# A decoder layer on one core: four banks shared by row maxima and scores, all heads' scores as one group, and a new order of work on every engine

## The reference

```python
x = _layernorm(x + _L0_attn_ref(x, L0_attn_W_q, L0_attn_W_kv, L0_attn_W_o), axis=-1)
x = _layernorm(x + _L0_xattn_ref(x, ctx_2048, ctx_2048), axis=-1)
x = _layernorm(x + _L0_ffn_ref(x, L0_ffn_weight, L0_ffn_rram_variation), axis=-1)
```

## Time and profile before

| | us |
|---|---|
| median of 3 runs | 259.92 (259.2 to 260.36) |
| the profiled execution | 258.83 |
| its span, first to last instruction | 257.0 |
| TensorE busy | 197.5 (77%) |
| VectorE busy | 164.8 (64%) |
| GpSimd busy | 126.8 (49%) |
| ScalarE busy | 100.2 (39%) |
| mean granted clock of TensorE | 0.875 |

### The profile page before, as it was taken

How to read it: one execution, slowest core, us unless ns; L and a number is a source line. 1 busy time by engine, 2 the same in 40 slices (tenths; PEclk the granted TensorE clock), 3 DMA queues, 4 the chain that set the end, 5 groups by cost and what they waited for, 6 DMA issues and landing times.

```text
span 257.0 us, 4854 instructions
## 1 busy us (share of the span) xinstructions
PE 197.5 (77%) x1631; PEld 123.0 (48%) x1631; DVE 164.8 (64%) x398; ACT 100.2 (39%) x227; POOL 126.8 (49%) x272
## 2 busy tenths in 40 slices
PE   7827338997979797979797979797979787583721
PEld 4603124545646455646464646465655455343510
DVE  3473527388775867777767787758787766825141
ACT  1121111445444535455344536253726263323210
POOL 0421675776564645565646565536555553324311
PEclk9995755999997979999979999889999799859575
DMA  6516600002030303130303121213131100000000
GB/s 191 171 26 194 175 14 0 3 24 82 28 97 23 102 3 104 40 106 26 102 20 102 32 93 38 87 34 92 38 87 49 38 20 3 22 0 20 3 20 20
DMA packets 16840, 14.96 MB, mean 58 GB/s; under 512 B 2352, under 2 KB 14768, under 8 KB 16816
## 3 DMA queue, kind: packets, MB, share of 16 engines
q1 hardware_dynamic: 16816, 14.66, 18.6%
HBM read 12.55 MB, written 2.10 MB: 57 GB/s over the span
## 4 chain that ended last, share of the span: by engine, by line
PE 48%; POOL 16%; DVE 14%; issue 9%; ACT 9%; SPq 2%; DMA 2%; POOLq 0%; ACTq 0%; DVEq 0%
PE p_proj L373 9%; PE p_st L381 8%; PE p_out L390 8%; PE p_proj L482 6%; PE p_sum L507 5%; ACT probs L537 4%; DVE unit L697 4%; POOL probs L282 4%; PE p_ap L397 3%; PE p_st L521 2%; PE p_tr L513 2%; POOL nA L268 2%; DMA ident_s<-ident 2%; DVE x_b L611 2%; POOL rnA L275 1%
## 5 line engine op out<-in xcount | busy, mean ns | idle before, releaser
L282 POOL TENSOR_SCALAR_AFFINE_SELECT probs<-probs 128x512 f32<-128x512 f32 x64 | 41.2, 647 | 37.3 <-ACT probs L537 35.3
L537 ACT ACTIVATE probs<-p_st 128x512 f32<-128x512 f32 x64 | 38.0, 598 | 48.8 <-PE p_st L381 48.8
L632 DVE TENSOR_REDUCE x<-p_ap 128x4 f32<-128x512 f32 x64 | 43.7, 687 | 18.1 <-PE p_ap L397 18.1
L381 PE MATMUL p_st<-x1T,keys 32*128 32x128 f32 x512 | 39.0, 292 | 1.4 <-DVE att L650 1.4
L381 PEld LDWEIGHTS p_st<-x1T,keys 32*128 32x128 f32 x512 | 32.7, 194 | 5.4 <-issue 2.5
L251 POOL TENSOR_SCALAR ve<-mv 128x1 f32<-128x1 f32 x48 | 10.5, 219 | 44.4 <-DVE mv L627 44.3
L373 PE MATMUL p_proj<-w_in,xT_s 128*128 128x512 f32 x60 | 31.4, 650 | 0.0
L253 POOL TENSOR_TENSOR rstd<-ve,power 128x1 f32<-128x1 f32 x48 | 27.2, 567 | 4.0
L482 PE MATMUL p_proj<-w_ffn,xqT_s 128*128 128x256 bf16 x96 | 15.0, 299 | 15.4 <-DVE unit L697 12.0
L390 PE MATMUL p_out<-probs,vals 128*32 128x128 f32 x512 | 26.2, 334 | 0.6 <-POOL probs L282 0.6
L579 ACT ACTIVATE outT_s<-p_out 128x512 f32<-128x512 f32 x16 | 9.6, 597 | 39.6 <-PE p_out L390 39.6
(11 more groups left out here) (80 smaller groups left out, 305.0 us busy)
## 6 DMA issues: line engine op xcount, KB each, us to landing
vals<-ctxV SPq DMA_DIRECT2D x16, 256.0 KB, 2.8
xT_s<-xT SPq DMA_DIRECT2D x16, 128.0 KB, 2.5
x_s<-x SPq DMA_DIRECT2D x16, 128.0 KB, 2.8
keys<-ctxK SPq DMA_DIRECT2D x64, 32.0 KB, 2.2
out<-res SPq DMA_DIRECT2D x16, 128.0 KB, 1.7
wq_s<-w_q SPq DMA_DIRECT2D x1, 256.0 KB, 3.0
dft_s<-dft SPq DMA_DIRECT2D x1, 256.0 KB, 3.2
wkv_s<-w_kv SPq DMA_DIRECT2D x1, 256.0 KB, 4.3
```

The lines of the kernel that those rows point to most:

```text
L282: nc.gpsimd.affine_select(out=part, in_=part, compare_op=ALU.is_ge, fill=0.0, base=0, pattern=[[0, GH], [1, TOK]], channel_multiplier=-1). ...
L381: mm = nc.tensor.matmul(p_st[s % 2][:, g * TOK:(g + 1) * TOK], keys[t.b % 4][slot, GH * g + s, :], x1T[slot, g, :], start=True, stop=True)
L537: nc.scalar.activation(probs[:, c, :, :].rearrange("p g q -> p (g q)"), p_st[c % 2][:], ACT.Exp, scale=HD ** -0.5).then_inc(exps[c], 1)
L632: nc.vector.tensor_reduce(x1[(t.b + 1) % 4][:, GH * c:GH * (c + 1), HD], p_ap[c % 2][:].rearrange("p (h k) -> p h k", h=GH), AX.X, ALU.max ...
```

## The change

The four chunks get one bank each, `p_b`, which serve the approximate products and then the scores of the next stage. `score` is one call for all 16 heads, with slot s in row group s and bank s. The FFN moves to `p_tr`, and the output's transposes go back into `p_out`. The output's transpose, the two exponentials of a pair and most other pieces get another place: each engine's `step` is written anew, with other offsets (`steps(step, ahead, behind)`), so that a batch passes from its projection to its output in seven steps of TensorE instead of five. The refinement of the norms is one square on ScalarE and two instructions on VectorE (`hA`, `rnA`) instead of four on GpSimd. GpSimd fills all four key tiles and casts the constants; ScalarE copies the folded output weights, whose fold stands behind the first projection. SP's queue stores first, then loads xT and x, then keys and values.

```diff
-        p_st = [bank(f"p_st{i}", [128, CW]) for i in range(2)]
-        p_ap = [bank(f"p_ap{i}", [128, CW]) for i in range(2)]
+        p_b = [bank(f"p_b{c}", [128, CW]) for c in range(CHUNKS)]
...
+        p_ffn = p_tr[:, 0:2, :].rearrange("p a b -> p (a b)")
...
-            for b in range(BATCH + 1):
-                load_and_store(Step(b), b + 4 < BATCH, b + 3 < BATCH, b > 0)
+            def step(t):
+                if t.has(-4):
+                    sp.wait_ge(out_ready, t.done(-3))
+                    sp.dma_start(out[t.batch(-4)], res[t.ring(-4, 2)][:]).then_inc(stored[t.ring(-4, 2)], 16)
+                if t.has(4) and t.batch(4) >= 4:
                     sp.wait_ge(proj, t.done(1))
+                    load_xT(t.batch(4))
                     sp.wait_ge(added[0], t.done(1))
+                    load_x(t.batch(4))
+                if t.has(1) and t.batch(1) >= 4:
+                    sp.wait_ge(pv_done[1], t.done(-2))
+                    load_kv(t.batch(1))
...
+            def score(buf):
+
+                for g in range(GROUPS):
+                    for s in range(GH):
+                        slot = slice(SLOT * s, SLOT * (s + 1))
+                        last = nc.tensor.matmul(p_b[s][:, g * TOK:(g + 1) * TOK], keys[buf][slot, GH * g + s, :],
+                                                x1T[slot, g, :], start=True, stop=True)
+                last.then_inc(scored, 1)
...
+                if t.has(1):
+                    dve.wait_ge(rsA_squared, t.done(2))
+                    nc.vector.scalar_tensor_tensor(out=hA[:], in0=nA[:], scalar=-0.5, in1=ssq[:], op0=ALU.mult,
+                                                   op1=ALU.mult).then_inc(half_step, 1)
...
+                    dve.wait_ge(half_step, t.done(2))
+                    nc.vector.scalar_tensor_tensor(out=rnA[:], in0=hA[:], scalar=1.5, in1=rsA[:], op0=ALU.add,
+                                                   op1=ALU.mult).then_inc(rnA_done, 1)
```

More of the change, by code:

```diff
@@ L57, in has, with steps @@
         return 0 <= self.b + off < BATCH
-def steps(step):
-    for b in range(-3, BATCH + 1):
+def steps(step, ahead, behind):
+    for b in range(-ahead, BATCH + behind):
         step(Step(b))
@@ new lines, in step @@
+                if t.has(0):
+                    if t.batch(0) == 0:
+                        pe.wait_ge(in_ident, 16)
+                    pe.wait_ge(y_done, t.done(1))
+                    for g in range(2):
+                        last = nc.tensor.transpose(p_sum[:, 1, g * TOK:(g + 1) * TOK],
+                                                   y[:, GH * 2 * g:GH * 2 * (g + 1), :, :]
+                                                   .rearrange("p h i k -> p (h i k)"), ident_s[:])
+                    last.then_inc(yT, 1)
@@ new lines, in step @@
+                if t.has(-2):
+                    pe.wait_ge(maxed[0], t.done(-1))
+                    pe.wait_ge(x1T_b_copied, t.done(0))
+                    for g in range(GROUPS):
+                        last = nc.tensor.transpose(p_tr[:, g, :], x1[t.ring(-2, 4)][:, GH * g:GH * (g + 1), :]
+                                                   .rearrange("p h s -> p (h s)"), ident_s[:])
+                    last.then_inc(x1T_done, 1)
+                if t.has(-1):
+                    pe.wait_ge(kv_in[t.ring(-1, 4)], t.filled(-1, GH + 1, 4))
+                    pe.wait_ge(x1T_b_copied, t.done(0))
+                    approximate(t.ring(-1, 4), 1)
@@ new lines, in step @@
+                if t.has(0):
+                    if t.batch(0) == 0:
+                        pe.wait_ge(w_out_ready, 1)
+                    pe.wait_ge(yT_copied, t.done(1))
+                    for g in range(2):
+                        last = nc.tensor.matmul(p_sum[:, 0, :], yT_s[:, g, :], w_out[:, g, :],
+                                                start=(g == 0), stop=(g == 1))
+                    last.then_inc(outA, 1)
+                if t.has(-3):
+                    pe.wait_ge(outT_copied, t.done(-2))
+                    for g in range(GROUPS):
+                        last = nc.tensor.transpose(p_out[:, g, :], outT_s[:, g, :], ident_s[:])
+                    last.then_inc(out_done, 1)
@@ new lines, in step @@
+                if t.has(-4):
+                    pe.wait_ge(xq_done, t.done(-3))
+                    pe.wait_ge(x1T_copied, t.done(-1))
+                    for g in range(2):
+                        last = nc.tensor.transpose(p_trb[:, g, :], xq[:, g * 128:(g + 1) * 128], ident_b[:])
+                    last.then_inc(xqT, 1)
+                if t.has(-2):
+                    pe.wait_ge(x1T_copied, t.done(-1))
+                    pe.wait_ge(maxed[1], t.done(0))
+                    score(t.ring(-2, 4))
@@ new lines, in step @@
+                if t.has(-1):
+                    pe.wait_ge(exps[2], t.done(-1))
+                    approximate(t.ring(-1, 4), 2)
+                if t.has(-4):
+                    if t.batch(-4) == 0:
+                        pe.wait_ge(ffn_seq, 10)
+                    pe.wait_ge(xqT_copied, t.done(-3))
+                    for g in range(2):
+                        for i in range(3):
+                            last = nc.tensor.matmul(p_ffn, xqT_s[:, g, :], w_ffn[i][:, g, :],
+                                                    start=(g == 0 and i == 0), stop=(g == 1 and i == 2))
+                    last.then_inc(ffn, 1)
@@ L445, in step @@
-                if t.has(1):
-                    pe.wait_ge(x1T_b_copied, t.done(2))
-                    pe.wait_ge(kv_in[(t.b + 1) % 4], t.filled(1, GH + 1, 4))
-                    approximate(t, 0)
-                    approximate(t, 1)
-                if t.has(2):
-                    pe.wait_ge(yT_copied, t.done(3))
-                    for g in range(2):
-                        last = nc.tensor.matmul(p_sum[:, 0, :], yT_s[:, g, :], w_out[:, g, :],
-                                                start=(g == 0), stop=(g == 1))
-                    last.then_inc(outA, 1)
@@ L526, in _ @@
+            steps(step, 2, 4)
         @block.scalar
@@ L736, in dft_tables @@
+            steps(step, 1, 5)
 def dft_tables():
```

647 lines of the change are left out of this document (276 added, 371 removed).

## The result

The changed kernel takes 209.89 us (median of 4 runs, 207.78 to 212.08) against 259.95 us before: a ratio of 0.805 (95% interval 0.798 to 0.812), 50 us less where 42 were forecast. On another chip, later, it took 209.04 us (0.794, 0.788 to 0.801).

What follows compares the result with a forecast made beforehand. TensorE was taken as nearest to full (10.38 of 12.00 us), VectorE second. First FFN 67.5, nine full steps 91.8, four lighter 37.2, to last FFN 12.4, to span's end 6.8, outside 1.8: 217.5, so 218 us; range 206 to 238.

Steps and rivals of the forecast that it cites:

- Scores as one group: TensorE's 32 score instructions in four row groups take 1.2 us, cutting its work by 1.1 us a step.
- rival B: Row groups don't load weights side by side: the score group takes 1.9 us, total 229 us; chance 0.20.
- TensorE's loop of 9.92: TensorE's step: 10.38 us busy, less 1.1 for the scores, plus 0.64 of waiting, makes 9.92 us.
- The new wait: On TensorE, the next approximate matmul waits for the exponential of chunk 2: 0.60 us plus 0.04 of signals.
- VectorE: VectorE gains hA and rnA at 0.2 us each: 9.41 + 0.4 = 9.8 us a step, nearly TensorE's.
- I let them cancel: On VectorE, xq's possible saving of 0.3 us is offset by another instruction meeting a GpSimd mask.
- The loads: The loop through SP's queue and the key and value loads takes 9.55 us, hidden by 0.4 us only.
- no wait for a key or value load shows: Sign in the changed profile: no such wait before TensorE's approximate matmul of chunk 1.
- rival C: Loads land late or VectorE meets masks: 1.5 us in each of 14 steps, total 239 us; chance 0.13.
- The clock: TensorE's lower clock adds 0.3 us to each step, 9.9 to 10.2 us.
- rival D: TensorE's clock stays at its lower level most of the time: 275 us, slower than before; chance 0.05.
- Head: Start of the kernel: batch 0's y at 17.5 us, first FFN at 67.5, later than before through two extra steps.

Runs made afterwards that it cites:

- e1_keys_first: The changed kernel with SP issuing a step's keys and values ahead of the store, xT and x: 202.95 us, ratio 0.775.
- the one-edit run above: The kernel before the change, with GpSimd refining the norms between the masks of chunks 0 and 1 instead of behind both: 250.84 us, ratio 0.966.
- e4_ffn_prep_earlier: The changed kernel with GpSimd's three pieces of FFN preparation moved from the end of its step to behind y: 198.51 us, ratio 0.766.
- the last run of the chain of edits: The changed kernel with keys and values issued first, FFN preparation behind y, and FFN matmuls ahead of the approximate matmul of chunk 2: 188.45 us.

## Why the prediction was right, point by point

**The sum**, in its own terms, forecast and measured in the profiled execution: first FFN 67.5 and 69.8; nine full steps 91.8 and 158.35 - 69.83 = 88.5; four lighter ones 37.2 and 32.6; to the last FFN 12.4 and 11.1; to the end of the span 6.8 and 6.7; outside it 1.8 and 1.7. The profiled execution took 210.4 us, 7 less than that sum: 3.3 of it lie in the full steps, 4.6 in the lighter ones and 1.3 on the way to the last FFN, and 2.3 in the head go the other way. That the full step came within 0.4 us of its 10.2 is partly luck. Two terms were too long, TensorE's loop by 0.66 us (9.92 for 9.26) and the clock by 0.3; the loads, taken for hidden, put back 0.58 (9.26 to 9.84 in the mean).

**Scores as one group**: right, at 1.17 us for 1.2, and for the reason given, row groups that work side by side; rival B is out. The Trainium skill's 107 ns a load (TensorE: Matmul & The Clock Gate, LDWEIGHTS) fails only if it is taken across row groups, as the prediction said: the 32 loads take 0.98 us here, not 3.4. Within one row group it holds: eight of the loads go to each, (0.98 - 0.187) / 7 = 0.113 us apart, an estimate that takes the four to go in step. Two row groups show the same, with 16 loads in 0.97 us. So the 0.052 us between loads, from which the prediction made its bound of 1.9 us, was no pace of a single load path: the 32 come 0.026 us apart.

**TensorE's loop of 9.92** was mis-sized: 9.26 (the first full step, and every one of e1_keys_first). The new wait was right, 0.64 forecast and 0.72 measured. The work was not: 8.5 us instead of 9.3. Busy time of before holds the end of each matmul that nothing follows at once; with fewer stops there are fewer such ends. Counted to the start of the next row, or to its own end where TensorE then idles, the four approximate matmuls of a step fell from 1.32 to 0.92 us, the weighing, now in one piece instead of two, from 1.16 to 1.02, and the FFN and the cumulative sum by 0.1 each: 0.7 together, beside the 1.1 of the scores.

**VectorE**: 8.8 us a step instead of 9.8. hA and rnA are 0.13 and 0.18 us in the median, 0.31 for the 0.4 forecast, and xq is 0.426 us in all 16 batches. "I let them cancel" was one failing step: it saved 0.3 and no meeting with a mask cost it back. That makes 9.4 us of the 9.8. The other 0.6 were missing from the sum altogether: the durations of a step's VectorE instructions add up to 10.6 us in both kernels, but busy time counts overlap once, and it fell from 9.41 to 8.8. A row whose follower doesn't need it is overlapped by some 0.08 us (L648 runs from 71.25 to 71.66 us, L651 starts at 71.58), and the new order has more such neighbours. The port rule of the Trainium skill (SBUF — State Buffer, Who interferes with whom), cited there, agrees with xq in the one-edit run above (0.734 us beside a mask, 0.426 without).

**The loads**: the loop was forecast at 9.55 us and is 9.45 to 9.59 where nothing is late. "It is hidden by 0.4 us only" was wrong, since it was compared with a TensorE loop 0.65 too long; it isn't hidden at all, it sets the step, and late issues make it 9.84 in the mean. So the sign "no wait for a key or value load shows" failed as well. This is rival C's mechanism at half a microsecond instead of 1.5.

**The clock**: 0.3 us a step forecast, none measured, and rival D didn't come.

**Head**: y of batch 0 was forecast at 17.5 us and the timeline has it at 18.6 (18.20 + 0.43); the first FFN came 2.3 us late. That the first FFN comes later than before although y comes sooner was right, but not the reason, two more steps of depth. With the FFN preparation elsewhere (e4_ffn_prep_earlier) the same depth has its first FFN at 57.5 us, 6.3 ahead of the kernel before.

## What to carry to other kernels

When several loops lie close together, work out each of them, with its transfers, and take the longest as the bound; then remove it and read the next, as the last run of the chain of edits does here: 209.9, 203.0, 193.0, 188.5 us. A queue that issues loads behind a wait for a result makes the loads part of that result's loop; issue them before it. Let matmuls of few rows go round all row groups: the same 32 instructions take 1.17 us in that order and 1.72 pair by pair. And don't read busy time as work: it fell by 0.7 us a step on TensorE and 0.6 on VectorE because stops and dependent neighbours went.

## What the runs showed of the hardware that I had not expected

An issue on SP's queue sometimes takes much longer than its 0.43 us. SP's queue in the changed kernel:

```profile
97.41 1.02 SPq L171 DMA_DIRECT2D xT_s<-xT  x1
...
107.55 1.50 SPq L171 DMA_DIRECT2D xT_s<-xT  x1
```

The steps in which this happened are 10.1 to 10.7 us long instead of 9.5. With the keys first the same kernel has such issues (1.51 us once) and steps of 9.27 beside them. What holds them up wasn't tried.

A row group took the same time for its matmuls and their weight loads with two at work or four: eight instructions in each (32 rows, 128 columns) took 1.16 and 1.17 us.

And with a change of 0.6 us in the order of GpSimd, worth 0.3 us a step by itself, the profiled execution shows no drop of TensorE's clock in its first ten full steps, where the kernel before has four. Whether the edit did that, one trace of each can't show. Where the clock falls now and then, compare the steps at the full clock before you put a price on a small edit.
